# One weighing of all heads per step, a ring of four PSUM banks, and a residual summed in place

## What is computed

```python
x = x + tanh(g_xattn) * attention(layernorm(x), ctx)   # 16 heads of 32, causal, softmax, w_q w_k w_v w_o with biases
x = x + tanh(g_ffn) * (dequant(fp6_blocks(layernorm(x))) @ wd.T + bias)   # blocks of 32, wd quantised alike
```

## Time and profile before

| | |
|---|---|
| median of 3 runs | 1426.57 us (1426.28 to 1427.3) |
| the profiled execution | 1426.4 us, span 1424.4 us |
| PE busy | 1381.7 us (97% of the span), 10844 matmuls |
| DVE busy | 1102.1 us (77%) |
| ACT busy | 894.7 us (63%) |
| POOL busy | 854.3 us (60%) |
| chain that ended last | PE 91%, DVE 3%, the rest 2% or less each |
| mean granted TensorE clock | 0.989 |

### The profile page before, as it was taken

The page is one execution under the profiler, slowest core; times in us unless marked ns, Lnnn a source line. Parts: engine busy times, 40 slices in busy tenths (PEclk is TensorE's granted clock), DMA queues, the critical chain, the costliest instruction groups (busy, mean ns, idle before and its releaser), DMA issues.

```text
span 1424.4 us, 35124 instructions
## 1 busy us (share of the span) xinstructions
PE 1381.7 (97%) x10844; PEld 1220.1 (86%) x10844; DVE 1102.1 (77%) x4219; ACT 894.7 (63%) x2969; POOL 854.3 (60%) x1387
## 2 busy tenths in 40 slices
PE   6899999999999999999999999999999999999976
PEld 6788888888888888888888888888888888888865
DVE  5778787887788878778788778788778887877763
ACT  4566666666666666666666666666666666666651
POOL 2455665566665666666656566556666566666662
PEclk9999999999999999999999999999999999999988
DMA  8444434444434444434444443444443444443310
GB/s 255 107 112 106 117 93 120 115 128 107 119 90 118 118 125 118 108 94 116 118 119 124 108 114 97 116 117 128 107 119 93 115 117 125 118 111 90 86 51 29
DMA packets 156103, 159.10 MB, mean 112 GB/s; under 512 B 28176, under 2 KB 130576, under 8 KB 155920
## 3 DMA queue, kind: packets, MB, share of 16 engines
q1 hardware_dynamic: 155920, 156.87, 41.6%
HBM read 39.33 MB, written 16.78 MB: 39 GB/s over the span
## 4 chain that ended last, share of the span: by engine, by line
PE 91%; DVE 3%; SPq 2%; issue 1%; ACT 1%; POOL 1%; DMA 1%; DVEq 0%; ACTq 0%; POOLq 0%
PE proj L483 20%; PE proj L484 20%; PE proj L485 20%; PE pT_ps L533 12%; PE oT_ps L550 6%; PE proj L577 6%; PE s_ps L522 4%; PE s_ps L523 2%; SPq L342 1%; DMA all_probs<-in_L_xattn_w_v 1%; ACT all_probs L660 1%; DVE all_probs L807 0%; DMA q_stack<-q_hi 0%; POOL x L448 0%; POOL x L444 0%
## 5 line engine op out<-in xcount | busy, mean ns | idle before, releaser
L410 POOL TENSOR_TENSOR all_probs<-all_probs,rden 128x128 f32<-128x128 f32 (+1 forms) x1024 | 505.0, 514 | 473.3 <-DVE rden L867 472.1
L660 ACT ACTIVATE all_probs<-all_probs,neg_max 128x128 f32<-128x128 f32 (+1 forms) x1024 | 458.7, 451 | 396.7 <-DVE neg_max L807 396.5
L807 DVE CUSTOM_DVE_ANT_0 all_probs<-s_ps,causal 128x128 f32<-128x128 f32 (+1 forms) x1024 | 321.7, 351 | 164.4 <-PE s_ps L523 160.8
L533 PE MATMUL pT_ps<-ident,all_probs 128*128 128x128 f32 x1536 | 264.5, 282 | 6.6 <-POOL all_probs L410 4.3
L660 ACT ACTIVATION_READ_ACCUMULATOR all_probs<-all_probs,neg_max 128x1 f32 x1024 | 195.5, 191 | 0.0
L919 DVE COPY all_probs<-pT_ps 128x384 f32<-128x384 f32 x256 | 139.0, 543 | 66.5 <-PE pT_ps L533 66.5
L533 PEld LDWEIGHTS pT_ps<-ident,all_probs 128*128 128x128 f32 x1536 | 160.4, 142 | 21.7 <-issue 12.7
L522 PE MATMUL s_ps<-k_stack,q_stack 96*128 96x256 f32 x512 | 154.8, 302 | 2.8 <-DVE neg_max L807 2.2
L483 PE MATMUL proj<-cT_hi,wk_hi 128*128 128x256 f32 x512 | 153.2, 299 | 1.9 <-DVE cT_lo L861 1.1
L483 PE MATMUL proj<-aT_hi,wq_hi 128*128 128x256 f32 x512 | 148.0, 289 | 0.4 <-ACT vs L675 0.4
L484 PE MATMUL proj<-cT_lo,wk_hi 128*128 128x256 f32 x512 | 142.4, 278 | 0.0
(11 more groups left out here) (125 smaller groups left out, 3487.3 us busy)
## 6 DMA issues: line engine op xcount, KB each, us to landing
k_stack<-k_hi SPq DMA_DIRECT2D x512, 64.0 KB, 2.0
q_stack<-q_hi SPq DMA_DIRECT2D x512, 64.0 KB, 2.1
xs<-in_x SPq DMA_DIRECT2D x32, 512.0 KB, 4.2
cs<-in_ctx SPq DMA_DIRECT2D x32, 512.0 KB, 6.1
k_stack<-k_lo SPq DMA_DIRECT2D x256, 64.0 KB, 2.0
q_stack<-q_lo SPq DMA_DIRECT2D x256, 64.0 KB, 2.1
out<-x SPq DMA_DIRECT2D x32, 512.0 KB, 3.0
vs<-in_L_xattn_w_k SPq DMA_DIRECT2D x2, 512.0 KB, 7.0
```

What stands on the lines that cost most here:

```text
L410: last = nc.gpsimd.tensor_tensor(p, p, rden[:, sd, t, h:h + 1].to_broadcast([P, (1 + t) * P]), ALU.mult)
L533: last = nc.tensor.transpose(pT_ps[h % 2][:, m * P:(m + 1) * P], probs[:, h % P_RING, m * P:(m + 1) * P], ident[:, :])
L660: last = nc.scalar.activation(probs[:, h % P_RING, cols], probs[:, h % P_RING, cols], ACT.Exp, scale=-1.0, bias=neg_max[:, sd, t, h:h + 1] ...
L807: last = nc.vector.tensor_tensor_reduce(probs[:, h % P_RING, cols], s_ps[h % 2][:, cols], causal[:, (1 - t) * P:], 1.0, MASKED, ALU.add, A ...
```

## The change

The values of all 16 heads are weighed in one block, in slot 3, three steps behind (lag 3); `probsT` has 16 places. The bank of the weighing joins the three others: every unit, each of the two halves of the weighing (av, eight heads each) and once the bias takes the next of four banks, strictly in turn (`taken`, `place_of`, `bank_of`); TensorE waits for the user four places earlier (`free_bank`). `SLOT_PARTS` is changed: slot 3 holds no part of a unit, k's fourth part moves to slot 4 in front of dT's second half, and the parts of slots 10 to 14 shift. x1 is gone: o and f are added in place to x in its ring, which has five places; the x load waits for the output of five batches earlier, and the output goes as two half DMAs. xn of batch i moves from slot 15 of step i to slots 2 and 3 of step i+1. SP waits for head 15's maxima of the previous batch before it stacks k's second half. In step 34, the last but one, o of the last batch stands in front of f of the batch before it (`LAST_O`). Cut to its core:

```diff
-AV_LAG = 11
-
-OUT_SLOTS = ((AV_LAG + 1) % SLOTS, (AV_LAG + AV_HEADS + 1) % SLOTS)
+AV_SLOT = 3
+AV_STEPS = 3
...
-BANKS = (0, 1, 2, 0, 1, 2, 0, 1, 2, 0, 1, 2, 0, 1, 0, 2)
+LAST_O = ((1, ("dT", 0)), (4, ("dT", 1)), (4, ("o", 0)), (5, ("o", 1)), (9, ("f", 0)), (10, ("f", 1)))
+BANKS = 4
 PARTS = {"cT": 1, "xT": 1, "dT": 1, "q": 4, "k": 4, "v": 4, "o": 4, "f": 4}
-SLOT_PARTS = (2, 4, 4, 1, 1, 5, 4, 2, 3, 4, 4, 1, 3, 3, 3, 2)
+SLOT_PARTS = (2, 4, 4, 0, 2, 5, 4, 2, 3, 4, 3, 3, 3, 3, 2, 2)
...
-XN_SLOT = SLOTS - 1
-X_RING = 4
+XN_SLOTS = (2, 3)
+X_RING = 5
...
+    lag_of = {(kind, half): lag for kind, half, lag in UNITS}
+
+
+    work = {}
+    for i in range(STEPS):
+        if i == B + 2:
+
+            for s, (kind, half) in LAST_O:
+                work.setdefault((i, s), []).extend((kind, half, i - lag_of[kind, half], p) for p in range(PARTS[kind]))
+        else:
+            for (u, part), s in zip(usual, slot_of):
+                kind, half, lag = UNITS[u]
+                if live(i - lag):
+                    work.setdefault((i, s), []).append((kind, half, i - lag, part))
+
+    taken = []
+    for i in range(STEPS):
+        for s in range(SLOTS):
+            if s == AV_SLOT and live(i - AV_STEPS):
+                taken += [("av", r, i - AV_STEPS) for r in range(2)]
+            taken += [(kind, half, b) for kind, half, b, part in work.get((i, s), ()) if part == 0]
+            if (i, s) == (1, ADD_SLOT):
+                taken.append(("bias", 0, 0))
+    place_of = {who: n for n, who in enumerate(taken)}
...
-        all_probs = sb("all_probs", [P, P_RING + AV_HEADS, 3 * P])
+        all_probs = sb("all_probs", [P, P_RING + HEADS, 3 * P])
...
-        proj = [pb(f"proj{n}") for n in range(max(BANKS) + 1)]
+        proj = [pb(f"proj{n}") for n in range(BANKS)]
         s_ps = [pb(f"s_ps{n}") for n in range(2)]
         pT_ps = [pb(f"pT_ps{n}") for n in range(2)]
-        oT_ps = pb("oT_ps")
...
+        def finished(i, s, ago=1):
+
+            n = SLOTS * i + s - ago
+            for kind, half, b, part in work.get((n // SLOTS, n % SLOTS), ()):
+                if part == PARTS[kind] - 1:
+                    yield kind, half, b
+
+        def bank_of(kind, half, b):
+            return proj[place_of[kind, half, b] % BANKS]
+
+        def bank_before(kind, half, b):
+
+            n = place_of[kind, half, b] - BANKS
+            return taken[n] if n >= 0 else None
...
+                    if some(n := HEADS * (i - 2)):
+
+                        sp.wait_ge(max_ok, n)
                     sp.wait_ge(left["k"], 2 * (i - 2) + 2)
                     stack("k", i - 2, 1)
                 if live(i):
-                    if some(n := 2 * i):
-                        sp.wait_ge(xn_ok, n)
+                    if i == 1:
+                        sp.wait_ge(xn_ok, 2)
+                    elif 1 < i < X_RING:
+
+                        sp.wait_ge(wT_done, KC * len(WEIGHTS))
+                    elif i >= X_RING:
+
+                        sp.wait_ge(out_moved, 16 * T * (i - X_RING + 1))
...
-                    sp.wait_ge(left["f"], 2 * (i - 4) + 2)
-                    sp.dma_start(batch_of(out, i - 4), x1[:, side(ph, 4), :, :]).then_inc(
-                        x1_moved[side(ph, 4)], 16)
+                    for half in range(T):
+                        sp.wait_ge(left["f"], 2 * (i - 4) + half + 1)
+                        sp.dma_start(out[i - 4, half * P:(half + 1) * P, :], xs[:, place(ph, 4), half, :]).then_inc(
+                            out_moved, 16)
...
+            def free_bank(kind, half, b):
+
+                before = bank_before(kind, half, b)
+                if before and before[0] == "av":
+                    pe.wait_ge(olo_ok, 2 * before[2] + before[1] + 1)
+                elif before and before[0] == "bias":
+                    pe.wait_ge(add_ok, 1)
+                elif before:
+                    pe.wait_ge(left[before[0]], 2 * before[2] + before[1] + 1)
...
-            def weigh_values(b, r, sd):
-
-                pe.wait_ge(pT_even, 8 * b + 4 * r + 4)
-                pe.wait_ge(pT_odd, 8 * b + 4 * r + 4)
+            def weigh_values(b, sd):
+
+                pe.wait_ge(pT_even, 8 * b + 8)
+                pe.wait_ge(pT_odd, 8 * b + 8)
                 pe.wait_ge(left["v"], 2 * b + 2)
-                if some(n := 2 * b + r):
-
-                    pe.wait_ge(olo_ok, n)
-                for half in range(2):
-                    for kt in range(T):
-                        for j in range(GROUP):
-                            d = (AV_HEADS * r + GROUP * half + j) * DK
-                            last = nc.tensor.matmul(
-                                oT_ps[j * DK:(j + 1) * DK, half * S + kt * P:(half + 1) * S], vs[:, sd, kt, d:d + DK],
-                                probsT[:, GROUP * half + j, 2 * P * kt:2 * P + P * kt], start=kt == 0,
-                                stop=kt == T - 1, tile_position=(0, j * DK))
-                last.then_inc(av_done, 1)
-
-            def unit(u, part, kind, half, b, i):
-                bank = proj[BANKS[u]]
-                if part == 0 and (before := bank_before(u, i)):
-
-                    pe.wait_ge(left[before[0]], before[1])
+                for r in range(2):
+                    free_bank("av", r, b)
+                    bank = bank_of("av", r, b)
+                    for half in range(2):
+                        for kt in range(T):
+                            for j in range(GROUP):
+                                h = AV_HEADS * r + GROUP * half + j
+                                last = nc.tensor.matmul(
+                                    bank[j * DK:(j + 1) * DK, half * S + kt * P:(half + 1) * S],
+                                    vs[:, sd, kt, h * DK:(h + 1) * DK],
+                                    probsT[:, h, 2 * P * kt:2 * P + P * kt], start=kt == 0,
+                                    stop=kt == T - 1, tile_position=(0, j * DK))
+                    last.then_inc(av_done, 1)
+
+            def unit(kind, half, b, part):
+                bank = bank_of(kind, half, b)
+                if part == 0:
+                    free_bank(kind, half, b)
...
-                    if s % AV_HEADS == AV_LAG % AV_HEADS:
-                        lag = 2 if s >= AV_LAG else 3
-                        if live(i - lag):
-                            weigh_values(i - lag, (s - AV_LAG) // AV_HEADS % 2, side(ph, lag))
+                    if s == AV_SLOT and live(i - AV_STEPS):
+                        weigh_values(i - AV_STEPS, side(ph, AV_STEPS))
                     lag, b, h = transposed_head(i, s)
                     if live(b):
                         transpose_probs(b, h)
-                    units(i, s)
+                    for kind, half, of, part in work.get((i, s), ()):
+                        unit(kind, half, of, part)
...
-                        output_hi(i - 3, 1)
-                    if s == OUT_SLOTS[0] and live(i - 2):
-                        output_hi(i - 2, 0)
+                    for kind, half, of in finished(i, s):
+                        unit(kind, half, of)
+                    if s == AV_SLOT + 1 and live(i - AV_STEPS):
+                        for r in range(2):
+                            output_hi(i - AV_STEPS, r)
...
-                    dve.wait_ge(x1_moved[sd], 16 + 8 * b - 8 * sd)
-                    nc.vector.tensor_tensor(x1[:, sd, half, :], bank[:, :], xs[:, pl, half, :],
-                                            ALU.add).then_inc(left["o"], 1)
+                    nc.vector.tensor_tensor(x1[:, half, :], bank[:, :], x1[:, half, :], ALU.add).then_inc(left["o"], 1)
...
+            def normal_rows(b, t):
+
+                dve.wait_ge(rs1, b + 1)
+                if some(n := 2 * b):
+
+                    dve.wait_ge(done["xT"], n)
+                nc.vector.tensor_scalar(xn[:, t, :], xs[:, b % X_RING, t, :], mom1[:, t, 0:1], rstd1[:, t:t + 1],
+                                        ALU.subtract, ALU.mult).then_inc(xn_ok, 1)
...
+                    if s in XN_SLOTS and i > 1 and live(i - 1):
+                        normal_rows(i - 1, XN_SLOTS.index(s))
...
-                        if some(n := 2 * b + h // AV_HEADS):
-
-                            dve.wait_ge(av_done, n)
-                        nc.vector.tensor_copy(probsT[:, h % AV_HEADS, :], pT_ps[0][:, 0:3 * P]).then_inc(pT_even, 1)
+                        if some(b):
+
+                            dve.wait_ge(av_done, 2 * (b - 1) + h // AV_HEADS + 1)
+                        nc.vector.tensor_copy(probsT[:, h, :], pT_ps[0][:, 0:3 * P]).then_inc(pT_even, 1)
...
+                    if s == AV_SLOT + 1 and live(i - AV_STEPS):
+                        for r in range(2):
+                            output_lo(i - AV_STEPS, r)
```

More of the change, by code:

```diff
@@ L210, in fused_kernel @@
         c_in = sem("c_in")
[L212 removed]
+        out_moved = sem("out_moved")
         stacked = {k: [[sem(f"{k}_stacked{n}_{e}") for e in range(2)] for n in range(2)] for k in "qk"}
```

(54 more changed lines are left out.)

94 lines of the change are left out of this document (43 added, 51 removed).

## The result

The changed kernel takes 1523.06 us (median of 4 runs, 1521.33 to 1529.25) against 1426.93 us of the kernel before (4 runs, 1426.28 to 1427.80): ratio 1.0681, 95% interval 1.0650 to 1.0712. It is 96 us slower; the forecast was +113 us (1539, range 1484 to 1560). The profiled execution is the slowest of the four, 1529.25 us with a span of 1527.5; the mean granted clock is 0.958 in it and 0.963 in the others.

What follows compares the result with a forecast made beforehand. The prediction took TensorE, busy 40.47 of 40.50 us, to bound the kernel. From 1426.4 us it added 87 (wait) and 40 (clock), and took off 6 (block), 6 (last steps) and 2 (first steps): 1539.4 us, range 1484 to 1560.

Steps and rivals of the forecast that it cites:

- The bank order: Slot 5: f0 takes k0's bank and waits 3.0 us for k_lo in 29 steps, +87 us (75 to 99).
- Rival B: f0 does not wait, as VectorE's list ahead of k_lo shrinks from 4.6 to 1.6 us: 1412 us; chance 8%.
- The race: From slot 3's first transpose (time zero), k_lo ends at 5.5 us, f0 wants to start at 2.5: wait 3.0 us.
- I went through all 18: Of 18 bank users a step, 17 have a whole slot after the earlier user's end; only f0 has not.
- The clock: Behind f0's waits, 25 of 29 gaps bring TensorE's clock down at 1.6 us each: +40 us (0 to 49).
- The merged block: One weighing block less per step saves 0.2 us in 31 steps: -6 us (-3 to -10).
- Two gains put at nothing: Edits including the moved xn were put at nothing, +-4 us in all; no gain from cT0's new bank was named.
- Last steps: End of the program: last o starts 4.5 us sooner, last weighing costs +1.44 us; together -6 us (0 to -9).
- First steps: Steps 2 and 3: xT0 no longer takes k0's bank, so its wait there goes: -2 us (-3 to +3).
- The sum: Whole kernel: 1426.4 + 87 + 40 - 6 - 6 - 2 = 1539.4 us.

Runs made afterwards that it cites:

- `k_slot3`: The changed kernel with k's fourth part back in slot 3, f0 still taking k0's bank: 1428.32 us, ratio 1.0010 to the kernel before.
- `swap`: The changed kernel with f0 and xT0 exchanging banks in the ring, program order untouched: 1415.23 us, ratio 0.9909 to the kernel before.
- `before_k4`: The kernel before with k's fourth part in slot 4 instead of slot 3, banks by the old table: 1432.15 us, ratio 1.0033.
- `before_wait`: The kernel before with k's fourth part in slot 4 and f0 taking k0's bank in its table of three: 1535.33 us, ratio 1.0749.
- `best`: `both` with VectorE doing aT_lo of dT0 ahead of the copy of head 0 in slot 3: 1400.21 us, ratio 0.9809 to the kernel before.
- `both_split`: `both` with the weighing of 16 heads cut into two blocks of eight by the transposes of slot 3: 1410.60 us.
- `both_f_first`: `both` with the last batch's o again behind f of the batch before it, as in the kernel before: 1413.70 us.
- `both`: `swap` with the first half of the weighing read out one slot earlier, in slot 3: 1405.46 us, ratio 0.9845 to the kernel before.

## Why the prediction was right, and where not

- **The bank order.** Right in its main point: f0 behind k0, because of bank and slot together, once in each of 29 steps, put down to k_lo, and no other wait over 5 us in the steady part of the matmuls' list (the weight loads' has one of 5.5, dT1's). `k_slot3`, `swap`, `before_k4` and `before_wait` show it from four sides. Rival B had asked for 1.6 us of list ahead of k_lo; VectorE never stood, as the rows after show.
- **The race.** k_lo's end: worked out 5.5 us after time zero, measured 5.41. f0's wish: worked out 2.5, measured 2.74 (722.17 - 719.43). So the wait was 2.73 us instead of 3.0, and the term +79 instead of +87. The step that failed is "I went through all 18. Seventeen have at least one whole slot". dT1 has one too, but its bank's earlier user, dT0, is read out in slot 3, where VectorE first waits for the weighing and then copies head 0: aT_lo ends at 721.17 and dT1 starts at 721.22, 0.2 us late. A slot between is enough where VectorE is abreast of TensorE, and slot 3 is where it is not. `best`, whose step is 0.24 us shorter, shows the price.
- **The clock.** +40 expected, 36 measured by the medians. In the profiled execution there were fewer falls than forecast (22, not 25) and each was dearer (1.9 us on the mean, not 1.6). The Trainium skill, "TensorE: Matmul & The Clock Gate", section "A second HAM failure mode: psum-queue depth-cycling", says that short idle stretches between groups make the clock go up and down, and the prediction read it as a fall behind every gap. Here it fell in 22 of 29 gaps of 2.50 us, in 15 of 29 of 2.40 us and in 14 of 29 of 2.62 us (`before_wait`). So the runs agree with the kind of thing; counting all 29 would have been too many (and 4 falls more at 1.6 us are 6 us, not the 8 of the prediction). The share of 25 in 29 was a guess from two lone idle times, 1.79 (no fall) and 2.35 (fall) in the earlier trace rows; it came near for this kernel and would have been far off for `before_wait`, so its closeness is in part luck.
- **The merged block.** -0.2 us a step expected. The slots that the block's move touches (3, 4 and 10 to 15), added up from scores to scores, take 19.44 us before and 19.20 in `best`, where dT1 does not wait: -0.24. Right; and `both_split`, in which cutting the block lengthens slot 3 by 0.31, has the same sign and size. The Trainium skill, "TensorEngine Tiling (Array Packing)", section "Key Properties", says that a change of tiling mode drains TensorE; the sign agrees, and the whole saving of one block, entry and exit, is some 0.24 us here.
- **Two gains put at nothing.** From scores to scores slot 0 takes 1.53 us before and 1.32 in most steps after, slot 2 3.35 and 3.09. TensorE's own list of waits before does not show what went, since the delays lie within the modelled end of the transposes ahead; the waits of its weight loads do (200 to 1350 us, before, and then after, where both rows are gone and dT1's has come):

```profile
PEld proj L577 <- DVE k_lo L835: 6.6, 27, 0.5
PEld proj L483 <- DVE cT_lo L861: 6.2, 26, 0.2
```

```profile
PEld proj L617 <- DVE aT_lo L890: 5.5, 25, 0.2
```

  The first, 0.21 us in slot 0, is a gain of the ring, which the prediction overlooked. Before, cT0 takes k1's bank (both have a 0 in `BANKS`) and stands until k_lo is done (713.40 to 714.28, cT0 at 714.34); in the ring it takes q0's, long read out. xn has no part in it, since it stands on VectorE behind that k_lo. The prediction had gone through the 18 for what the ring makes late, and not for what it makes early.

  The second, 0.26 us in slot 2, fits the moved xn, which had been put at nothing, within +-4 us, and comes to -8 here. xn in slot 15 had stood on VectorE ahead of cT's low part, which the k matmuls of slot 2 wait for. Before, the two xn (714.20 to 715.78) pushed VectorE's list back, cT_lo ended at 719.54 and the first k matmul followed at 719.68, 6.03 us behind slot 0's scores; after, cT_lo ended at 713.04, 1.4 us earlier in the step, and k started at 714.21, waiting for nothing, 5.64 us behind them. In 31 steps 0.26 us are 8 us. The cause is read from two traces that differ in much else; no run moves xn alone. I had looked for what hides the moved operations in their new place, and not for what they held up in the old one.
- **The ends.** Last steps -6 expected: from the last weighing to the end 35.9 us before and 31.2 after, but the step ahead of it took 33.9 instead of 33.5 us; about -4. Taking the last o away again costs 4 to 8 us (`both_f_first`). First steps -2 expected (-3 to +3): the weighing of step 3 begins at 90.25 us before and at 85.59 after, -4.7. Part of it may be the two small gains again; no run separates them.
- **The sum.** From 1426.9: wait 29 x 2.73 = +79; clock +36; the steps otherwise -12 (42.25 down to 42.11 of `swap` less its 0.27 of wait, times 29: -0.41 a step. In the usual step cT0's bank -0.21, cT_lo -0.26, the block -0.24 and dT1 +0.24 make -0.47; against it, some steps are up to 1 us longer in slot 15 after the change, where the next scores wait for the copies into `q_stack` by DMA, under 0.1 on the mean); start -5; end -4. This gives 1521; measured 1523. The forecast was 16 too high: 8 by the wait, 4 by the clock and 7 by the rest, less the 2 to 3 that stay open here. In the rest, the two gains put at nothing (14 us) outweigh dT1's wait, which was put at nothing too (7 us). The three errors have one sign, and the range took them in.

## What to carry to other kernels

When buffers are handed out in turn, write down for every user the time at which the reader of the previous content ends and the time at which the new user wants to start, both in the order of the reader's own queue. A count of places or slots between them is not a distance in time: here one exchange of two neighbours in the list of users was worth 108 us, and another reader's place in its queue 0.24 us a step.

When an operation is moved away from a place, or a buffer gets another earlier user, price what stood there as well as what it will hold up in its new place. And when a part is taken back to measure its price, look whether the step gained elsewhere: the cut block cost 0.31 us and showed as 0.07. In a dense stream of matmuls such a delay shows in the distance from start to start and in the waits of the weight loads, and not in the matmuls' own list.

## What the runs showed of the hardware

- A single idle stretch of 2.4 to 2.6 us of TensorE in an otherwise dense stream brings the granted clock to the lower level in some steps and not in others: 15 of 29 at 2.40 us, 22 of 29 at 2.50, 14 of 29 at 2.62, so not in the order of their length. A fall costs 1.6 us in `before_wait` and 1.9 us on the mean in the kernel after (43 us by 22).
- Keeping TensorE at work over the gap with eleven matmuls whose result is dropped gives the clock's 36 us back, and the wait stays.
- A block of matmuls on tiles of 128 by 32, cut in two with transposes of 128 by 128 between, costs 0.31 us more than in one piece (slot 3 of `both_split` and `both`, 3.62 and 3.31 us).
- The engine that reads out first and the one that reads out second were 0.1 us apart in their claim on the end (k_hi and k_lo). Once the one is relieved the other sets the same time: 0.6 us off VectorE's list gave 0.1 us.
